# Attention of a four-layer block: where the projections and weight splits stand in the order, and extra whole-array products ahead of narrow scores

## The reference

```python
q = (x @ Wq.T + bq).reshape(b, l, h, hd).transpose(0, 2, 1, 3)   # h = 32 heads of hd = 16
k = (x @ Wk.T + bk)...; v = (x @ Wv.T + bv)...
scores = jnp.einsum('bhqd,bhkd->bhqk', q, k) / math.sqrt(hd)
scores = jnp.where(causal, scores, -jnp.inf)
att = jax.nn.softmax(scores, axis=-1)
out = jnp.einsum('bhqk,bhkd->bhqd', att, v)...
return out @ Wo.T + bo
```

## Time and profile before

| | us |
|---|---|
| median of three runs | 4295.83 |
| the profiled execution | 4294.83 |
| its span | 4293.1 |
| TensorE busy | 3861.4 |
| VectorE busy | 2711.2 |
| GpSimd busy | 1880.8 |
| ScalarE busy | 1695.2 |
| eight quads, first element | 347.07 |
| eight quads, second element | 341.38 |

### The profile page before, as it was taken

How to read it: one execution, slowest core, us unless ns; L and a number is a source line. 1 busy time by engine, 2 the same in 40 slices (tenths; PEclk the granted TensorE clock), 3 DMA queues, 4 the chain that set the end, 5 groups by cost and what they waited for, 6 DMA issues and landing times.

```text
span 4293.1 us, 61464 instructions
## 1 busy us (share of the span) xinstructions
PE 3861.4 (90%) x18056; PEld 2813.5 (66%) x18056; DVE 2711.2 (63%) x5034; ACT 1695.2 (39%) x3538; POOL 1880.8 (44%) x2017
## 2 busy tenths in 40 slices
PE   7899799689999999979878896996899999999797
PEld 4444478567777777757654444885677777777576
DVE  3567445577777777764435673555777777777644
ACT  1344411355545555541113444113555555555411
POOL 1111344355555655654311113443555556655542
PEclk8677899899999999989977767998999999999899
DMA  3221011011100111001032210110101001110010
GB/s 73 36 36 31 24 51 45 22 33 30 32 20 25 34 32 29 22 15 45 35 81 36 36 32 29 46 45 22 35 28 32 20 25 34 32 29 22 15 52 35
DMA packets 81456, 145.59 MB, mean 34 GB/s; under 512 B 16392, under 2 KB 18520, under 8 KB 81264
## 3 DMA queue, kind: packets, MB, share of 16 engines
q1 hardware_dynamic: 81264, 143.28, 12.9%
HBM read 113.08 MB, written 4.19 MB: 27 GB/s over the span
## 4 chain that ended last, share of the span: by engine, by line
PE 69%; issue 11%; DVE 7%; ACT 4%; POOL 3%; DVEq 2%; POOLq 2%; DMA 1%; SPq 1%; ACTq 0%
PE banks L492 15%; PE banks L493 14%; PE banks L494 14%; PE banks L832 4%; PE banks L671 4%; PE banks L652 3%; PE banks L628 3%; PE banks L825 2%; PE banks L845 2%; DVE conv L1344 2%; DVEq L1347 1%; PE banks L767 1%; PE banks L768 1%; POOL X L1509 1%; ACT conv L1005 1%
## 5 line engine op out<-in xcount | busy, mean ns | idle before, releaser
L1344 DVE SCALAR_TENSOR_TENSOR conv<-banks,cpar,conv 128x509 f32<-128x509 f32 (+2 forms) x576 | 428.2, 744 | 115.3 <-ACT conv L1005 100.9
L948 ACT ACTIVATE probs<-banks 128x1024 f32<-128x1024 f32 (+3 forms) x384 | 297.7, 810 | 309.4 <-PE banks L652 308.9
L1172 DVE TENSOR_TENSOR Y<-banks,Y 128x512 f32<-128x512 f32 x400 | 276.1, 691 | 188.1 <-PE banks L494 187.9
L1608 POOL TENSOR_SCALAR_AFFINE_SELECT probs<-probs 128x256 f32<-128x256 f32 x256 | 104.2, 408 | 645.8 <-ACT probs L948 645.5
L628 PE MATMUL banks<-stack_k,stack_q 48*128 48x512 f32 (+3 forms) x768 | 331.7, 502 | 59.3 <-DVEq L1218 19.8
L1672 POOL TENSOR_TENSOR state<-state,gt 128x512 f32<-128x512 f32 x112 | 133.5, 1192 | 500.4 <-PE banks L825 500.4
L492 PE MATMUL banks<-xhi,f_hi 128*128 128x512 f32 x800 | 322.6, 403 | 3.5 <-DVE xlo L1143 3.5
L492 PE MATMUL banks<-xhi,wx_hi 128*128 128x512 f32 x768 | 312.0, 406 | 14.4 <-DVE conv L1344 14.4
L493 PE MATMUL banks<-xhi,f_lo 128*128 128x512 f32 x800 | 319.9, 400 | 0.0
L494 PE MATMUL banks<-xlo,f_hi 128*128 128x512 f32 x800 | 319.4, 399 | 0.0
L494 PE MATMUL banks<-xlo,wx_hi 128*128 128x512 f32 x768 | 306.0, 398 | 0.0
(11 more groups left out here) (209 smaller groups left out, 10185.0 us busy)
## 6 DMA issues: line engine op xcount, KB each, us to landing
m_raw<-in_w_mamba SPq DMA_DIRECT2D x224, 256.0 KB, 2.6
f_raw<-in_w_ffn SPq DMA_DIRECT2D x50, 768.0 KB, 4.5
stack_q<-part_hi SPq DMA_DIRECT2D x128, 64.0 KB, 2.4
stack_k<-part_hi SPq DMA_DIRECT2D x128, 64.0 KB, 2.5
X<-in_x SPq DMA_DIRECT2D x4, 1024.0 KB, 6.5
wqk_raw<-in_w_attn SPq DMA_DIRECT2D x8, 512.0 KB, 3.5
stack_q<-part_lo SPq DMA_DIRECT2D x64, 64.0 KB, 2.4
stack_k<-part_lo SPq DMA_DIRECT2D x64, 64.0 KB, 2.5
```

What stands on the lines that cost most here:

```text
L948: act.activation(probs[n % 2][:, 2 * p:2 * p + 2, 0:w], banks[:, 2 * p:2 * p + 2, 0:w], ACT.Exp, scale=1.0 / HD ** 0.5).then_inc(exp_done[ ...
L1172: dve.tensor_tensor(Y[:, i, :], bank[6 + i % 2], Y[:, i, :], ALU.add).then_inc(f["dn_used"], 1)
L1344: r = dve.scalar_tensor_tensor(out=rest, in0=src[:, 0:HALF - lag], scalar=cpar[:, o:o + 1], in1=rest, op0=ALU.mult, op1=ALU.add)
```

## The change

There are three edits. A new entry `split_w` of the order carries the split of a weight slice, which so far hung on use 0 of its projections: slice 0 ahead of everything, slice 1 before piece 9 of quad zero, slice 2 after step 4 of quad zero, slice 3 after step 4 of quad two. The projections of slices 2 and 3 are placed after steps 1 and 3 of quads one to four, two per quad: slice 2 in quads one and two, slice 3 in quads three and four. And TensorE makes an extra product of the whole array (128 rows, 128 columns, 512 moving columns of `xhi`) into the bank of scores 0 and 2 ahead of them, in steps 9 to 11 of every quad and in steps 1 to 3 of quads 0, 5, 6 and 7; the score that follows overwrites it. SyncE's program is not in the diff.

```diff
--- before.py
+++ after.py
@@ -282,11 +282,14 @@
 
         def attention_order():
 
+            yield "split_w", 0
             for use in range(4):
                 yield "proj", 0, use
             for i in range(5):
                 yield "values_in", i
             for n in range(NP):
+                if n == 9:
+                    yield "split_w", 1
                 if n in (3, 9, 15):
                     yield "values_in", 5 + (n - 3) // 6
                 if n in (21, 27, 33, 39):
@@ -313,8 +316,10 @@
                         yield "turn", t - 1, 1
                     if n == 7:
                         yield "turn", t, 0
-                    if t % 2 and n < 8 and n % 2 and (t + 3) // 2 < NQ // 2:
-                        yield "proj", (t + 3) // 2, n // 2
+                    if 1 <= t < 5 and n in (1, 3):
+                        yield "proj", (t + 3) // 2, n // 2 + 2 * (t % 2 == 0)
+                    if t in (0, 2) and n == 4:
+                        yield "split_w", t // 2 + 2
                 yield "values", t, NS - 1
             yield "turn", NQ - 1, 1
 
@@ -649,6 +654,8 @@
                             pe.wait_ge(mt_in, START + (b * NQ + t + 1) * 32)
                         if h % 2 == 0:
                             pe.wait_ge(exp_done[h // 2], START + it)
+                        if lo and h % 2 == 0 and (n >= CPH or t in (0, NQ - 3, NQ - 2, NQ - 1)):
+                            pe.matmul(bank[h][:], xhi[:, 0, 0:P], xhi[:, 0, 0:HALF], start=True, stop=True)
                         r = pe.matmul(bank[h][:, 0:HALF - lo],
                                       stack_k[buf][base:base + ROWS + 2, h, j * P:(j + 1) * P],
                                       stack_q[buf][base:base + ROWS + 2, h, s * HALF + lo:(s + 1) * HALF],
@@ -1581,13 +1588,10 @@
                 ring = 0
                 for what, *arg in ORDER:
                     if what == "proj":
-                        f, use = arg
                         ring += 1
-                        if use < 3 and use > 0:
-                            continue
-                        if use == 3:
-                            wqk_last_use = ring
-                            continue
+                        wqk_last_use = ring
+                    elif what == "split_w":
+                        f, = arg
                         held(pool, wqk_in, (b * (NQ // 2) + f + 1) * 32)
                         if f > 0:
                             held(pool, ring_done, b * RING + wqk_last_use)
```

## The result

The changed kernel takes 4385.82 us (median of 4 runs, 4355.85 to 4396.18), the kernel before 4296.44 beside it (4293.31 to 4315.62). The ratio is 1.0191, interval 1.0155 to 1.0226: slower by 82 us by this ratio and by 89 between the two medians, where 64 were forecast. The median lies 27 us above the 4359 predicted and 0.8 above the end of the range.

What follows compares the result with a forecast made beforehand. TensorE, busy 3861.4 of 4293.1 us with much attention work at the low clock, was taken as the bound. Element one's +31.3 us and element two's +32.5, together 64 on 4294.83, gave 4359; range 4312 to 4385.

Steps and rivals of the forecast that it cites:

- SyncE's queue: Quads two and four: 48 stacking DMAs start later, so TensorE waits some 10 us for maxima; +21.5 and +23.6 us.
- E: End of the fourth projection of a slice, 24.7 us into quad two; quad three can begin at E + 38.1.
- The rival without a wait: A faster queue leaves no wait at the end of quads two and four; 4321 us, chance 0.13.
- Spread projections: Two projections each in quads one to four: quad one -7.4 us, three -5.5, two +21.5, four +23.6, queue wait included.
- Splits ahead: Quads one and three: TensorE's wait for the weight split hides in maskless steps; gain 1.7 us twice per element.
- Extra products: Full-array products in 36 steps per element cost their exposed time but raise the clock, worth 6 us per quad.
- The exposed price at the full clock: Steps 9 to 11 of each quad: six products show between 0 and 1.4 us; 0.75 taken.
- Quad zero: Starts at the low clock, pays 2.6 us, gets 3.5 from the clock and pays 0.75: -0.2.
- Quad seven: Taken as mostly high in clock already, so extra products cost +1.0 us.
- The rival of products that buy no clock: The gains of quads zero, five, six and seven, some 12 us per element, go; 4383 us, chance 0.13.
- The rival on the other side: TensorE stays at 2.4 GHz from step 0 through all quads; 38.6 us less per element, 4282 us, chance 0.09.
- the signs that the prediction named: Maxima waits some 10 us; quads two, four near 62, one, three near 53; no split wait; quads zero, six above 0.7.

Runs made afterwards that it cites:

- Experiment 3: The changed kernel with SyncE putting the maxima of quads three and five between the two stackings; 4354.21 us, ratio 1.0121 to the kernel before.
- experiment 7: The changed kernel with stacking DMAs of quads four to seven copying half the columns, same number of DMAs; 4386.56 us, ratio 1.0182 to the kernel before.
- experiment 1: The changed kernel without its 144 extra products, projections spread and splits ahead kept; 4340.59 us, ratio 1.0103 to the kernel before.
- experiment 4: The kernel before with only the weight splits moved ahead; 4287.19 us over 10 runs, ratio 0.9975.
- 2: The kernel before plus the 144 extra products, projections and splits in their old places; 4344.56 us, ratio 1.0091.
- experiment 8: The kernel before with splits ahead and slices 2 and 3's projections after steps 4 to 7 of quads one and three; 4291.92 us, ratio 0.9962.
- experiment 5: The kernel before with splits ahead and extra products only in steps 1 to 3 of quads five and six; 4285.29 us, ratio 0.9946.
- 12: The kernel before with splits ahead, projections in steps 4 to 7 of quads one and three, extras in steps 1 to 3 of five and six; 4287.21 us, ratio 0.9955.
- 6: The kernel before with splits ahead and extra products only in steps 9 to 11 of all quads; 4336.9 us, ratio 1.0060.
- 9: The kernel before with splits ahead, extras in steps 1 to 3 of quads five and six and steps 4 and 5 of seven; 4292.0 us, ratio 0.9972.
- 10: The kernel before, splits ahead, extras in steps 1 to 3 of quads five, six and steps 4, 5 of zero, two, four, seven; 4297.97 us, ratio 0.9991.
- 11: The kernel before with splits ahead and all 144 extra products cut to 128 moving columns; 4328.72 us, ratio 1.0062.

## Why the prediction was right and wrong

**The bound and the sign: right.** The attention of both elements holds the loss, and the kernel is slower. The total is nearer than its parts, and that is luck: the splits and the spreading were 60 us in the forecast and are 44, the extra products were 4 and are 38, and the two errors partly cancel.

**SyncE's queue: right, and near in size.** Place, cause and length hold: waits of 8.9 to 12.3 us at the four scores named, quad three 38.98 after E where 38.1 was worked out. Experiment 3 removes the wait by order alone and moves the time by 30 us; experiment 7 shows that the bytes don't set the spacing. The rival without a wait falls. The row was not as even as the prediction says: 0.63 us is the usual distance, and 32.4 us for 48 DMAs is 0.68 on average.

**Spread projections: right in sign, too dear by 8 us per element.** Quad one took 51.47, not 53.1; its first four steps are 1.85 + 7.86 + 4.46 + 8.22 = 22.39, not 27.60 - 1.7 = 25.9, and those of quad two 22.27, not 24.7. The two beginnings that the prediction went by held more of the low clock: step 2 of quad one took 5.40 us at 0.78 before and 4.46 at 1.00 here. In quad two the clock came at step 6, so its own work after E was 38.98 - 12.26 = 26.7, not 28.2; the longer waits come from that. Together, splits and spreading are 44 us by experiment 1, for both elements: -11 for the splits (experiment 4) and +55 for the rest (1.0103 / 0.9975).

**Splits ahead: right, and perhaps a little small.** 1.7 us twice per element, 7 us in all, against 11 with an interval from 0 to 22. No wait for a split is left ahead of slices 2 and 3.

**Extra products: here the prediction failed.** Its term was 4 us; experiments 1 and 2 give 38 and 39. One reading behind it does not hold: "Full-array products do raise it" rested on quads one and three at 0.77 and 0.82, but quad four, without a projection, stands at 0.78 in the same. Three things were mis-sized.
- *The exposed price at the full clock.* 0.75 per quad was taken, with 1.4 as the most. It is 1.9 in quad five. The 0.24 us was the spacing within a row of projection products. Alone between other work an extra product puts 0.43 us between its start and the score's, and 0.31 of that shows, though VectorE is busy for 80% of these steps.
- *Quad zero.* Six products at 0.60 us instead of 0.43 for steps 0 to 3, and the clock came no sooner than before (step 8; before, step 8 and step 7 in the two elements), so 3.5 us of gain were missing: 5.3 instead of -0.2.
- *Quad seven.* The largest miss, +16 for +1.0. The step was the words "mostly high already": that the clock was high was taken as a property of the quad. It is one of three ways in which this quad can run without any extra product in it: 26.7 us high from step 3 on, 34.3 low up to step 8 (experiment 4 shows both in one run), 38.6 low throughout (experiment 8). And the price of its twelve products was too small by the same error as above: even the two quads seven with all twelve and a clock of 0.89 to 0.90 (one element each of experiments 2 and 7) took 32.2 and 32.3 us.

**The rival of products that buy no clock** is half right: 4383 was near the 4386 measured, and true of quads zero and seven. It is not true of quad five (experiment 5) and not always of quad six: in the kernel after it took 34.47 us at 1.00 in the second element and 45.52 at 0.67 in the first, where 39.18 and 40.59 were the times before. The Trainium skill, page "TensorE: Matmul & The Clock Gate", section "What's actually happening", ties the throttle to how busy the array has been. Here quad zero was granted 0.64 with TensorE busy 45.60 of 46.17 us, so the busy share of the profile did not foretell the level.

**The rival on the other side**, a clock held throughout, falls: the quads one to four ran at 0.73 to 0.81. Of the signs that the prediction named, one failed in three of four places: the clock in quads zero and six was to be above 0.7, and it was 0.64 in both quads zero and 0.67 and 1.00 in quads six.

**What stays open.** What decides whether the clock returns in quads five to seven. Two elements of one run, with the same instructions, differ by 8 to 11 us in one quad. Quad seven is low up to step 8 or longer in 6 of the 12 profiled elements without extra products in it (before and experiments 1, 4, 5, 8 and 12), and has a mean clock of 0.64 or less in 14 of the 16 with them (the change and 2, 3, 6, 7, 9, 10, 11). That is a tendency and not a proof: 2 and 7 each have one element at 0.89 or 0.90, and in the whole kernel the loss by the extra products cannot be split into what they cost and what the clock would have done without them. Four products in its steps 4 and 5 don't end the low level (9). Why, no run here shows.

## What to carry to other kernels

When work that a DMA queue waits for is moved later, write down the whole row of DMAs that comes between it and the next transfer somebody needs: its number times the time of one, less what was to spare, is the wait. Reordering the queue can hand the wait to whoever owns the buffer behind it, so look at each such buffer. A filler product costs its own place on TensorE where TensorE is the engine that is never idle, at either clock, and a short one more than its share of columns; price it from where it will stand, not from a row of its like. A stage whose clock is high in one profile is not a stage that is always high: look at the other executions and the twin stage before giving it a small term.

## What the runs showed of the hardware

- Quad seven, with the same products, took 26.7, 34.3 or 38.6 us, at granted clocks 0.94, 0.65 and 0.51, without an extra product in it; with six more products it took 43.7 us at 0.51. TensorE was busy for 38.14 of the 38.62 us and still held at the low level.
- An extra product of 128 rows by 128 columns, alone between other work, cost 0.31 us with 512 moving columns and 0.17 with 128 at the full clock. At the low clock it cost 0.60 and 0.29 in quad zero, and 0.87 with 512 columns in the wide steps of quad seven.
- 48 DMAs from one queue took 33.2 us when each moved all the columns and 32.1 with half of them, most of them 0.63 us behind the one before.
